# An adaLN block with switch FFN on one core: raw modulation rows moved between the first maxima, the modulation weight in two transfers, identity products at the start

## What is computed

```python
mod = (silu(c) @ wmod).reshape(8, 6, 1, 256)          # c: 8 x 256, wmod: 256 x 1536
sa, ca, ga, sb, cb, gb = (mod[:, n] for n in range(6))
ga, gb = (sign(g) * maximum(abs(g), 0.25) for g in (ga, gb))   # sign(0) is 1
h = layernorm(x) * (1 + ca) + sa
x = x + ga * attention(h)      # q, k, v with bias, rope, causal softmax, Wo with bias
h = layernorm(x) * (1 + cb) + sb
x = x + gb * switch_ffn(h)     # each token through its best expert, times the probability
```

## Time and profile before

| | us |
|---|---|
| median of 3 runs | 870.07 |
| lowest and highest | 865.71, 870.69 |
| the profiled execution, its own time | 858.79 |
| its span, first to last instruction | 857.1 |
| mean granted TensorE clock in it | 0.942 of full speed |

### The profile page before, as it was taken

One profiled execution on the slowest core, in us unless ns is written; L12 is line 12 of the kernel. 1 busy time (PEld: TensorE's weight loads), 2 busy tenths in 40 slices (PEclk: granted clock), 3 DMA queues, 4 the chain that ended last, 5 costly groups with the idle time before them and its releaser, 6 DMA issues. The chain is left out here.

```text
span 857.1 us, 20563 instructions
## 1 busy us (share of the span) xinstructions
PE 733.5 (86%) x7252; PEld 431.0 (50%) x7252; DVE 628.3 (73%) x1279; ACT 492.6 (57%) x984; POOL 411.7 (48%) x530
## 2 busy tenths in 40 slices
PE   4957989999999999999998877311999999999994
PEld 3433444545444444545454333101777777777672
DVE  4766878988888989888887663690376766767674
ACT  1325788878787888888887775100434343444441
POOL 3313454767666676667675657401033333333331
PEclk9977999999999999999999999655899999999998
DMA  7040242336427225434443365597022222222200
GB/s 225 1 88 25 99 100 74 109 90 147 135 82 194 85 89 167 124 110 120 86 151 107 102 149 119 195 429 312 6 96 79 95 71 77 64 88 68 67 24 1
DMA packets 56183, 95.36 MB, mean 111 GB/s; under 512 B 6556, under 2 KB 39445, under 8 KB 55064
## 3 DMA queue, kind: packets, MB, share of 16 engines
q1 hardware_dynamic: 51000, 77.25, 30.1%
q0 software_dynamic: 4992, 16.79, 6.2%
q10 hardware_dynamic: 96, 0.01, 0.0%
HBM read 67.37 MB, written 34.50 MB: 119 GB/s over the span
## 5 line engine op out<-in xcount | busy, mean ns | idle before, releaser
L1026 DVE TENSOR_REDUCE row_max<-ps_max 128x2 f32<-128x1024 f32 (+2 forms) x192 | 200.1, 1042 | 38.7 <-PE ps_max L599 38.0
L854 ACT ACTIVATE prob<-ps_sc 128x1024 f32<-128x1024 f32 (+1 forms) x192 | 169.1, 881 | 61.4 <-PE ps_sc L626 58.8
L1486 PE MATMUL ps_h<-tok_t,w_all 128*128 128x128 f16 x1872 | 157.8, 222 | 2.9 <-issue 1.7
L1486 PEld LDWEIGHTS ps_h<-tok_t,w_all 128*128 x1872 | 133.1, 99 | 44.6 <-issue 5.8
L398 POOL TENSOR_SCALAR_AFFINE_SELECT prob<-prob 128x512 f32<-128x512 f32 x128 | 83.6, 653 | 121.9 <-ACT prob L854 121.7
L106 POOL DMA_INDIRECT slots<-row_dram,token x39 | 42.4, 1087 | 174.2 <-DVE y L1587 149.7
L1502 PE MATMUL ps_y<-w_all,hid_hi 128*128 x312 | 119.2, 383 | 0.9 <-DVE hid_lo L1573 0.9
L1542 ACT ACTIVATE hid<-ps_h,b_t 128x128 f32<-128x128 f32 x312 | 88.8, 371 | 50.3 <-PE ps_h L1486 50.2
L639 PE MATMUL ps_pv<-prob,v_sb 128*32 128x512 f32 (+3 forms) x1024 | 96.8, 451 | 0.0
L1533 ACT ACTIVATE tok_t<-ps_x 128x256 f16<-128x256 f32 x39 | 14.9, 383 | 140.2 <-PE ps_x L1471 140.2
L592 PE MATMUL ps_max<-k_t,q_t 64*128 64x256 f16 (+3 forms) x512 | 69.7, 310 | 18.8 <-DVE row_max L1026 12.8
(11 more groups left out here) (267 smaller groups left out, 1340.7 us busy)
## 6 DMA issues: line engine op xcount, KB each, us to landing
raw<-w SPq DMA_DIRECT2D x64, 256.0 KB, 3.2
w_dram<-halves SPq DMA_DIRECT2D x64, 256.0 KB, 3.4
w_all<-w_dram SPq DMA_DIRECT2D x8, 2048.0 KB, 23.8
row_dram<-rows SPq DMA_DIRECT2D x8, 1024.0 KB, 4.8
xs<-x SPq DMA_DIRECT2D x8, 512.0 KB, 5.2
rows<-x SPq DMA_DIRECT2D x8, 512.0 KB, 7.4
row_dram<-mods_dram SPq DMA_DIRECT2D x8, 512.0 KB, 9.9
mod_rows<-mods_dram SPq DMA_DIRECT2D x8, 384.0 KB, 10.6
```

Source lines behind the costliest of these rows:

```text
L854: nc.scalar.activation(p_kb[:, :, first * L:(first + n) * L], ps_sc[:, :, 0:n * L], ACT.Exp, scale=SCALE).then_inc(exp_done, 1)
L1026: nc.vector.tensor_reduce(dst, ps_max[:, :, 0:n * L].rearrange("p j (m l) -> p j m l", m=n), AX.X, ALU.max).then_inc(max_done, 1)
L1486: last = mm(o, w[:, :, k, f, :][:, bass.ds(e, 1), :].rearrange("p e m -> p (e m)"), tok_t[:, j % 2, part, k, :], start=(n == 0 and f % HF ...
```

## The change

Four things are changed:

1. 56 products of the f16 identity with itself into `ps_nd`, read by nobody, stand at the head of TensorE's list.
2. wmod is loaded in two transfers: parts 0 and 1 (512 KB) where the whole was, parts 2 to 5 (1024 KB) behind wo and ahead of sw.
3. The x transposes of tile 0 stand ahead of the modulation of parts 0 and 1.
4. The raw rows of parts 4, 3, 5 and 2 are made one at a time behind the first four of the six products of unit 0's maxima, in `ps_pv` and `ps_nd`. VectorE copies parts 4 and 3 after the third maximum and forms the gates after the negated maxima. SP's wait for them stands behind the first two expert pieces and xs of the third sequence, and ScalarE waits for the store before unit 1.

The core of the diff (on SP, the functions that only move are left out):

```diff
+WARM = 56
...
-            sp.dma_start(wmod_sb, wmod.rearrange("(c p) n -> p c n", p=P)).then_inc(mod_loaded, 16)
+            wmod_v = wmod.rearrange("(c p) n -> p c n", p=P)
+            sp.dma_start(wmod_sb[:, :, 0:2 * D], wmod_v[:, :, 0:2 * D]).then_inc(mod_loaded, 16)
             sp.dma_start(cos_t[:, :, :], rope_cos.rearrange("(t p) d -> p t d", p=P)).then_inc(rope_loaded, 16)
             sp.dma_start(sin_t[:, :, :], rope_sin.rearrange("(t p) d -> p t d", p=P)).then_inc(rope_loaded, 16)
             sp.dma_start(nat_o, wo.rearrange("(c p) i -> p c i", p=P)).then_inc(wo_loaded, 16)
+            sp.dma_start(wmod_sb[:, :, 2 * D:6 * D], wmod_v[:, :, 2 * D:6 * D]).then_inc(mod_rest_loaded, 16)
...
+            for m in range(2):
+                load_piece(m)
+            load_xs(2)
+            sp.wait_ge(mods_kept, 1)
             sp.wait_ge(gates_done, 1)
             sp.dma_start(mods_dram.rearrange("g b d -> b g d"), mod_r).then_inc(gates_saved, 16)
...
-            for m in range(2):
-                load_piece(m)
-            load_xs(2)
...
             pe.wait_ge(idents_done, 4)
-
+            for _ in range(WARM):
+                mm(ps_nd[:, 0:P], ident16[:, :], ident16[:, :], start=True, stop=True)
...
+            def raw_part(ps, n, part):
+
+                for k in range(KC):
+                    last = mm(ps[0:B, n * D:(n + 1) * D], c_t[:, k, :], wmod_sb[:, k, part * D:(part + 1) * D],
+                              start=(n == 0 and k == 0), stop=(k == KC - 1), skip_group_check=True)
+                return last
...
-            pe.wait_ge(ct_kept, 1)
-            pe.wait_ge(mod_loaded, 16)
-            modulation(0, ps_nd)
-
...
             x_transposes(0, ps_pv)
+            pe.wait_ge(ct_kept, 1)
+            pe.wait_ge(mod_loaded, 16)
+            modulation(0, ps_nd)
...
-                if T == 1:
-                    raw_mods(ps_max[:, 0, :])
-                if T == 2:
-                    raw_gates(ps_nd)
...
             for s in range(NSHOT):
                 max_scores(0, s)
+                if s == 0:
+                    pe.wait_ge(mod_rest_loaded, 16)
+                    raw_part(ps_pv, 0, 4)
+                if s == 1:
+                    raw_part(ps_pv, 1, 3).then_inc(mods_ps, 1)
+                if s == 2:
+                    pe.wait_ge(ht_done, KC * LEAD + KC)
+                    raw_part(ps_nd, 0, 5)
+                if s == 3:
+                    raw_part(ps_nd, 1, 2).then_inc(gates_ps, 1)
             shift_rows(0)
...
                     if s == 3:
+                        if U == 0:
+                            pe.wait_ge(mods_kept, 1)
                         weigh(U, 0)
...
                         if T + 1 < NT:
+                            if U == 0:
+                                pe.wait_ge(gates_kept, 1)
                             x_transposes(T + 1, ps_nd, U)
...
-            act.wait_ge(gates_saved, 16)
             keep_shift(0)
 
             for U in range(NU):
                 T, V, X, Z = U + LEAD, U + 1, U - QT, U - LAG
+                if U == 1:
+                    act.wait_ge(gates_saved, 16)
...
-                if T == 1:
-                    keep_mods()
-                if T == 2:
-                    keep_gates()
                 lo_parts(T)
             keep_qt(LEAD - 1, ps_b[:, :])
             modulate(LEAD, ps_nd)
             for s in range(NSHOT):
                 maxima(0, s)
+                if s == 2:
+                    keep_mods()
             negated(0)
+            keep_gates()
```

More of the change, by code:

```diff
@@ L235, in attention_part @@
         gates_ps, gates_done, gates_saved = sem("gates_ps"), sem("gates_done"), sem("gates_saved")
+        gates_kept, mods_kept, mod_rest_loaded = sem("gates_kept"), sem("mods_kept"), sem("mod_rest_loaded")
         gate_rows_saved = sem("gate_rows_saved")
@@ L290, in load_mods @@
                 sp.dma_start(mod_rows[:, b % 2, :, :], mods_dram[1:4, b, :].partition_broadcast(P)).then_inc(mods_loaded[b % 2], 16)
-            sp.wait_ge(gates_done, 1)
-            sp.dma_start(mods_dram.rearrange("g b d -> b g d"), mod_r).then_inc(gates_saved, 16)
-            sp.wait_ge(gates_saved, 16)
-            for b in range(2):
-                load_mods(b)
             def load_xs(b):
@@ L334, in _ @@
             load_xs(2)
+            sp.wait_ge(mods_kept, 1)
+            sp.wait_ge(gates_done, 1)
+            sp.dma_start(mods_dram.rearrange("g b d -> b g d"), mod_r).then_inc(gates_saved, 16)
+            sp.wait_ge(gates_saved, 16)
+            for b in range(2):
+                load_mods(b)
             for U in range(NU):
@@ L508, in modulation @@
                 last.then_inc(mod_ps, 1)
-            def raw_gates(ps):
-                for n, part in enumerate((5, 2)):
-                    for k in range(KC):
-                        last = mm(ps[0:B, n * D:(n + 1) * D], c_t[:, k, :], wmod_sb[:, k, part * D:(part + 1) * D],
-                                  start=(n == 0 and k == 0), stop=(k == KC - 1), skip_group_check=True)
-                last.then_inc(gates_ps, 1)
-            def raw_mods(ps):
-                for n, part in enumerate((4, 3)):
-                    for k in range(KC):
-                        last = mm(ps[0:B, n * D:(n + 1) * D], c_t[:, k, :], wmod_sb[:, k, part * D:(part + 1) * D],
-                                  start=(n == 0 and k == 0), stop=(k == KC - 1), skip_group_check=True)
-                last.then_inc(mods_ps, 1)
+            def raw_part(ps, n, part):
[3 more added lines that the diff above has]
+                return last
             pe.wait_ge(silu_done, 1)
@@ L954, in keep_gates @@
                 g = mod_r[:, 0:2, :]
-                link(nc.vector.tensor_copy(g, ps_nd[0:B, :].rearrange("p (g d) -> p g d", g=2)))
+                nc.vector.tensor_copy(g, ps_nd[0:B, :].rearrange("p (g d) -> p g d", g=2)).then_inc(gates_kept, 1)
+                dve.wait_ge(gates_kept, 1)
                 link(nc.vector.tensor_scalar(mod_s, g, 0.0, 2.0, ALU.is_ge, ALU.mult))
@@ L965, in keep_mods @@
                 dve.wait_ge(mods_ps, 1)
-                link(nc.vector.tensor_scalar(mod_r[:, 2, :], ps_max[0:B, 0, 0:D], 1.0, None, ALU.add))
-                link(nc.vector.tensor_copy(mod_r[:, 3, :], ps_max[0:B, 0, D:2 * D]))
+                link(nc.vector.tensor_scalar(mod_r[:, 2, :], ps_pv[0:B, 0:D], 1.0, None, ALU.add))
+                nc.vector.tensor_copy(mod_r[:, 3, :], ps_pv[0:B, D:2 * D]).then_inc(mods_kept, 1)
             def statistics(T):
```

## The result

| us | before | changed |
|---|---|---|
| median of 9 runs each | 867.67 | 860.81 |
| lowest and highest | 864.05, 870.69 | 857.41, 863.59 |
| the profiled execution, its own time | 858.79 | 860.67 |
| its span | 857.1 | 859.0 |
| mean granted TensorE clock in it | 0.942 | 0.940 |

The ratio of the medians is 0.9928, with a 95% interval of 0.9905 to 0.9951: 6.9 us faster, within 1% of no change. The forecast was 861.0, from a gain of 9.0.

The account below looks back on a forecast made before the run. TensorE and VectorE nearly fill the loop; the change touches the once-run lead-in, a chain of projections. Terms 3.1 + 0.6 + 1.8 + 1.45 + 1.7 + 0 + 0.3 = 9.0 us, off the median 870.07: 861, range 855 to 869.

Parts of the forecast that it names:

- Identity products: Head of TensorE's list: the 56 products end at 8 to 9 us, before the weights at 9.42, and cost nothing.
- Start to the first projection: Lead-in's beginning: the first projection starts at 15.7 us instead of 18.8, waiting for the bias rows; gain 3.1.
- First link: First to second projection, 6.99 us before: 6.4, with one clock fall charged at 1.7; gain 0.6.
- Second and third link: Next two projection-to-projection links, 14.07 us together: raw rows leave TensorE, VectorE sets the pace; gain 1.8.
- fourth: Link to the lead-in's last projection, 7.59 us: without the gates' operations on VectorE it takes 6.14; gain 1.45.
- last projection: Last lead-in projection to q transposes, 9.13 us: full instead of half rate gains 1.7, or 0 if the clock falls.
- Maxima of unit 0: First unit's maxima, now with the raw parts between: costs and savings sum to 0; ends -2 and +2.8 us.
- Gates and unit 1: Gates on VectorE after unit 0's negated maxima take back most of the clock's gain before unit 1; gain 0.3 us.
- The clock does not follow: Rival: TensorE starts at half rate as before or loses the clock elsewhere; gain 1.5 to 4.3 us, 867; chance 0.22.
- SP stalls again: Rival: the split transfer's second part stalls SP's queue, bias rows land at 19.2; gain 5.5, 864.6 us; chance 0.12.
- Slower: Rival: the lead-in falls to half rate, 4.2 us a link; all three links give 873.6 us; chance 0.08.
- Everything keeps full rate: Rival: full clock in the first link and unit 0's maxima too; gain 12.7, 857.4 us; chance 0.16.

Follow-up runs that it names:

- same_again: The changed kernel profiled once more with no edit; median 862.24 us, ratio 0.9947 to before.
- tail: The changed kernel with 8 more identity products behind each scores step of units 27 to 31; median 861.54 us, ratio 0.9939 to before.
- gates_off: The changed kernel with identity products in three idle places before unit 1, gates moved from VectorE to ScalarE and GpSimd; median 856.34 us, ratio 0.9878 to before.
- narrow_mix: The changed kernel with two identity products behind each modulation product but the last, 12 behind the whole; median 859.78 us, ratio 0.9919 to before.
- bridge: The changed kernel with 18 more identity products between the modulation and the first projection; median 862.42 us, ratio 0.9942 to before.
- raw_only: The kernel before with only the moved raw rows and gates, no identity products, wmod in one transfer; median 861.43 us, ratio 0.9949 to before.
- fill_all: The changed kernel with more identity products behind the modulation, before the last q transposes, in unit 0's maxima and in units 27 to 31; 859.20 us, ratio 0.9912.
- before_again: The kernel before profiled once more with no edit; 864.99 us in one run.
- ident_only: The kernel before with only the 56 identity products added; median 868.88 us, ratio 1.0042 to before.
- no_ident: The changed kernel without its 56 identity products; median 858.93 us, ratio 0.9919 to before.
- pool_early: gates_off with GpSimd's mask constants made earlier, one identity product behind each modulation product but the last, 12 behind the whole; 857.93 us, ratio 0.9891 to before.

## Why the prediction was right

Its time and its likeliest case came out, and so did the mechanism in the main: full rate for the modulation, an earlier start, links paced by VectorE. That the time came out as closely as it did is luck, as the last two steps show. This goes by its own steps, in the changed kernel's two traces.

- *Identity products: right.* Foreseen to end at 8 to 9, they ended at 8.06, at 0.108 us each, between my two rows of 0.129 and 0.077. The Trainium skill (TensorE: Matmul & The Clock Gate, Back-to-back issue gap) gave 107 ns and so 6.0 us; the trace, with 6.05, agrees. That they cost nothing is less sure: see the end of this section.
- *Start to the first projection: 3.1 forecast, 3.89 measured (3.0 in same_again).* Modulation at full rate 1.8 us foreseen, 1.85 measured, and h_t ready for a start at the foreseen 14.9. The bias rows bind beside it, as foreseen, but 15.7 is only one of the values they take: the last of them landed at 14.71 here, at 15.62 in same_again, 15.82 in tail and 15.53 in gates_off, with the projection 0.2 us behind each (the view names the load of sw in gates_off, but that had landed by 14.94). I had also kept wo's stall of 3.64 us behind a smaller transfer, and it was gone (0.51).
- *First link: 0.6 forecast, -0.7 measured (0.7 in same_again): the term that was most wrong.* I charged one fall at 1.7, that of a projection behind which the clock was up again: its v products took 1.13 us at 51.57. Here the clock was at half from the projection's first record to its v products (2.08 us at 19.45), and the link took 7.70, longer than the old 6.99, in which the clock rose in the v products (1.41 us at 23.34). The full price is 7.70 against the 4.60 of narrow_mix, 3.1 us. In same_again the fall came later and ended sooner (v products 1.13 us), the link took 6.25, and the charge of 1.7 held. And the idle time ahead of the projection, which I gave as the cause, isn't needed: bridge had none there and fell.
- *Second and third link: 1.8 forecast, 2.0 measured; fourth: 1.45 and 1.57; last projection: 1.7 and 1.69.* VectorE paced the links, as its rows had it (a copy q_t ahead of each projection), and the clock stayed. same_again has 2.0, 1.6 and 1.7, and raw_only shows these without the rest: 3.3 us by the last projection.
- *Maxima of unit 0: 0 forecast, 0.17 measured (-0.64 in same_again).* The raw parts cost 1.87 at half and 1.03 at full, as sized, and the clock rose one step sooner than in my sum. The stage took 11.97 us, and 12.78 in same_again, above the 12.3 that I had given as a sign of being wrong; the gain there hangs on when the clock rises.
- *Gates and unit 1: 0.3 forecast, 0.51 measured (-0.13 in same_again).* The maxima of unit 1 began at 63.57, where the gates ended (63.64). The half-rate projection (2.08 us at 62.66) hid part of them as I had it. gates_off gives the price of them with the clock up: 14.07 us in fill_all against 12.88, 1.2 us.
- *Moved transfers: nothing, right.* Nothing waits for them in the trace.
- *The sum: 9.0, measured 9.1 at unit 1 (8.2 in same_again).* Two terms were off by +0.8 and -1.3, the others by up to 0.2 each, nearly all in the good direction: the sum is better than its parts.
- *From the sum to the median: 9.0 subtracted, 6.9 measured (4.3 to 8.2 by the interval).* Here a step failed that I had not priced. I took one execution of before for all. Its start was a late one; before_again stands 1.9 us earlier at unit 1, and the gain between pairs of traces is 6.3 to 9.1. The forecast still met the median, since the 9.0 was taken from 870.07, the median of three runs, where nine give 867.67: an error of 2.4 in the start that met one of 2.1 in the gain. That is luck.

*One sign misfired.* I had called the forecast wrong if L550 took 3.7 us in the first two tiles. It took 3.78 in the first and 1.98 in the second, and the forecast held: my own sum had charged one such fall, so the first tile should not have stood in that sign.

**Rivals.** "The clock does not follow" was true of one link of five. "SP stalls again" was the opposite of what came. "Slower" is out: no later link was at half rate. "Everything keeps full rate" came nearest in fill_all, with three sets of fills before unit 1 and a first projection still at 3.55 us: 3 us better in the median. For warming as a whole the Trainium skill (TensorE: Matmul & The Clock Gate, Part 1) has under 1% of a typical span. The traces agree: 0.9 to 2.1 us at unit 1 of 859, 0.1 to 0.2%.

**What stays open.** Units 27 to 31 took 52.8 to 55.5 us in the ten traces of kernels with the 56 identity products at their head, and 51.6 to 52.6 in the four without (before, before_again, no_ident, raw_only). It fits the medians: ident_only is slower than before and no_ident is no slower than the changed kernel, though it is 0.9 to 2.1 us behind at unit 1. Yet the grouping was made after the traces were seen, the two ranges lie 0.2 us apart, most kernels have but one trace, and I have no mechanism by which products at 2 us lengthen units at 450. The clock is not it alone: tail, at 1.00, took 54.67, and before_again, at 0.93, 51.63. ScalarE's wait for the store of one weight piece is a part of it in some traces, 3.1 us in ident_only and 1.5 in no_ident, but none in tail. This was not settled. Nor was what makes the clock fall at the kernel's start: the same list of products kept it through the first projection in gates_off and lost it in bridge and fill_all. Nor was what sets the experts' 234.5 to 249.2 us, beyond that the gathers land at other times.

## What to carry to other kernels

Work that runs once before a full loop is worth moving when it stands between two others in the chain: the moved raw rows gave about 5 us behind the first projection in every trace that has them, and alone a median of 0.9949, with no trick of the clock. What the identity products and the split add is seen at the start of the traces, but not in the medians. Before a sum is subtracted from a median, profile the kernel before a second time: here its start moved by 2 us and an untouched stage by 8, as much as the whole change. And when an engine gets faster at a kernel's start, look at what the others still do there (GpSimd's constants) and at what stands behind the hidden work (the gates on VectorE), for that can take the gain next.

## What the runs showed of the hardware that I had not expected

- The granted clock fell while TensorE showed full busy time: in bridge to 0.50 from about 13.5, behind 16 products of 8 columns (1.87 us), as the wide ones behind them began; the last idle time, 0.99 us, had ended at 11.51. With wide ones mixed in it stayed up in narrow_mix and fell in pool_early, and without them it stayed up in gates_off through 1.07 us of idle time: the outcome differs between executions.
- The printed clock of before is 1.00 from 9.0 to 13.7, where its transposes take the half-rate 1.97 us; at a kernel's start the durations are what to go by.
- The time that SP needs to issue a transfer went with the bytes ahead of it: wo took 2.71 to 4.41 us behind 1536 KB of wmod (five traces), and 0.51 to 0.92 behind 512 KB (nine).
- The bias rows, 2 KB each, landed at different moments in executions of the same start: the last at 14.71 in the changed kernel, 15.62 in same_again, 15.82 in tail.
- An operation of 8x512 f32 on GpSimd takes 1.25 to 1.95 us; a copy of that shape took 0.59 on ScalarE and 0.67 on VectorE. The same step of two constants took 1.95 on GpSimd (gates_off) and 0.42 on VectorE (fill_all).
